# A hybrid block on one core: the x standardisation issued ahead of the magnitudes, and two VectorE side steps issued one head later

## What is computed

```python
def attention_a(x, Wq, Wk, Wv, Wo):          # x: (16, 512, 256), 16 heads of 16
    q, k, v = (split_heads(x @ W.T) for W in (Wq, Wk, Wv))
    scores = einsum('bhqd,bhkd->bhqk', q, k) * 16 ** -0.5
    scores = where(head_mask, scores, finfo.min)   # heads 0-7 strided, heads 8-15 fixed
    out = einsum('bhqk,bhkd->bhqd', softmax(scores), v)
    return out @ Wo.T

def ffn(x, w_gate, w_up, w_down):            # 256 -> 704 -> 256
    h = silu(fp4(x) @ fp4(w_gate).T) * (fp4(x) @ fp4(w_up).T)
    return fp4(h) @ fp4(w_down).T

def fp4(x):       # blocks of 16 along the last dimension
    scale = max(max(abs(block)) / 6, 1e-12)
    return nearest_of_grid(abs(block) / scale) * sign(block) * scale
    # grid: 0, 0.5, 1, 1.5, 2, 3, 4, 6

x = x + attention_a(layernorm(x)); x = x + ffn(layernorm(x))
x = x + attention_b(layernorm(x)); x = x + ffn(layernorm(x))
```

## Time and profile before

| | |
|---|---|
| runs of the kernel before | 3655.23, 3663.86, 3664.30 us (median 3663.86) |
| the profiled execution: its own time, its span | 3658.47 us, 3656.7 us |
| busy in the span: PE, DVE, ACT, POOL | 86%, 76%, 60%, 31% |
| attention A | about 45 to 1120 us |
| first feed-forward | about 1200 to 1770 us |
| attention B | about 1770 to 3065 us |
| second feed-forward | about 3150 to 3656 us |

### The profile page before, as it was taken

How to read it: one execution, slowest core, us unless ns; L and a number is a source line. 1 busy time by engine, 2 the same in 40 slices (tenths; PEclk the granted TensorE clock), 3 DMA queues, 4 the chain that set the end, 5 groups by cost and what they waited for, 6 DMA issues and landing times. The chain is left out here.

```text
span 3656.7 us, 70567 instructions
## 1 busy us (share of the span) xinstructions
PE 3141.8 (86%) x24024; PEld 2441.3 (67%) x24024; DVE 2772.7 (76%) x7209; ACT 2187.4 (60%) x5360; POOL 1121.8 (31%) x664
## 2 busy tenths in 40 slices
PE   6899899899895899997588888888888886699998
PEld 4666666666664788887356565566665654688888
DVE  4676676676666788886488888888878887688887
ACT  4666667676672344433477777877777775344343
POOL 1000000000003455554233333444333333455554
PEclk9999999999996999999699999999999897899999
DMA  5344244244332100000334344443443443110000
GB/s 89 43 68 61 43 68 61 44 68 61 51 49 75 47 18 18 18 12 29 52 50 68 59 69 66 68 72 59 64 71 59 69 60 87 41 35 30 29 30 24
DMA packets 134183, 190.46 MB, mean 52 GB/s; under 512 B 15127, under 2 KB 81559, under 8 KB 133143
## 3 DMA queue, kind: packets, MB, share of 16 engines
q1 hardware_dynamic: 133830, 185.95, 29.9%
HBM read 45.65 MB, written 28.84 MB: 20 GB/s over the span
## 5 line engine op out<-in xcount | busy, mean ns | idle before, releaser
L407 ACT ACTIVATE a_probs<-a_probs,a_negmax 128x176 f32<-128x176 f32 (+4 forms) x1024 | 501.7, 490 | 331.6 <-DVE a_negmax L330 331.2
L330 DVE CUSTOM_DVE_ANT_0 a_probs<-a_mask,a_score 128x176 f32<-128x176 f32 (+4 forms) x1024 | 404.0, 400 | 222.4 <-PE a_score L481 90.2
L492 PE MATMUL a_turned<-ident,a_probs 128*128 128x128 f32 (+1 forms) x2176 | 427.7, 289 | 79.3 <-DVE a_pT L339 71.6
L1716 DVE CUSTOM_DVE_ANT_0 b_u<-b_u,b_score 128x512 f32<-128x512 f32 x512 | 340.4, 681 | 137.2 <-PE b_score L1971 134.8
L1841 ACT ACTIVATE b_u<-b_u,b_negmax 128x512 f32<-128x512 f32 x512 | 367.0, 717 | 113.6 <-DVE b_negmax L1716 112.2
L1245 PE MATMUL f_y_bank<-f_wdT,f_hqT 128*128 128x256 f32 x1536 | 374.7, 396 | 60.2 <-ACT f_hqT L1184 60.2
L1708 DVE SCALAR_TENSOR_TENSOR b_u<-b_u,b_score 128x1024 f32<-128x1024 f32 x256 | 310.1, 1215 | 94.2 <-ACT b_u L1834 91.7
L1245 PEld LDWEIGHTS f_y_bank<-f_wdT,f_hqT 128*128 128x128 f32 x1536 | 296.4, 197 | 108.5 <-issue 67.9
L1834 ACT ACTIVATE b_u<-b_score 128x1024 f32<-128x1024 f32 x256 | 262.3, 1025 | 163.3 <-PE b_score L1961 163.0
L1177 ACT ACTIVATE f_h_mag<-f_hu 128x704 f32<-128x704 f32 x128 | 101.4, 792 | 421.2 <-POOL f_hu L1060 421.2
L1980 PE MATMUL b_turned<-ident,b_u 128*128 128x128 f32 x2048 | 322.1, 282 | 24.7 <-DVE b_pT L1722 19.4
(11 more groups left out here) (236 smaller groups left out, 7160.5 us busy)
## 6 DMA issues: line engine op xcount, KB each, us to landing
b_stack<-b_part SPq DMA_DIRECT2D x192, 256.0 KB, 8.4
a_stack_q<-a_part SPq DMA_DIRECT2D x192, 128.0 KB, 4.3
a_stack_k<-a_part SPq DMA_DIRECT2D x192, 128.0 KB, 5.7
xs<-in_x_dram SPq DMA_DIRECT2D x16, 512.0 KB, 8.2
x_before_b<-xs SPq DMA_DIRECT2D x16, 512.0 KB, 2.9
b_xin<-x_before_b SPq DMA_DIRECT2D x16, 512.0 KB, 12.2
b_xres<-x_before_b SPq DMA_DIRECT2D x16, 512.0 KB, 3.8
x_after_b<-b_xres SPq DMA_DIRECT2D x16, 512.0 KB, 5.8
```

Of the source, the lines that this page charges most:

```text
L330: dve.tensor_tensor_reduce(out=probs[:, n % 2, j, 0:keys(n)], in0=mask_of(n), in1=score[j][:, 0:keys(n)], scale=-1.0, scalar=3.0e38, op0=A ...
L407: act.activation(probs[:, n % 2, j, 0:keys(n)], probs[:, n % 2, j, 0:keys(n)], ACT.Exp, bias=negmax[:, n, j:j + 1], scale=-1.0, accum_out= ...
L492: m = nc.tensor.transpose(turned[j % 2][0:rows, u, :], chunk(n, probs[:, n % 2, j, :], u), ident[:])
L1716: dve.tensor_tensor_reduce(out=u[:, n, j, :], in0=u[:, n, j, :], in1=score[:, j, :], scale=-0.05, scalar=3.0e38, op0=ALU.add, op1=ALU.min, ...
```

## The change

Nothing is added or removed. In attention A, VectorE's share of the jobs Q, K and R is issued at head j = 2 instead of j = 1, behind `mask_max` and `move_turned` of that head; its share of V, y and xT1 stays at j = 1, and ScalarE's share of all jobs stays at j = 1. In both feed-forwards, ScalarE issues `magnitude` as the last part of a step, behind `scalar_magnitude` (n = 0) and `scalar_standard` (n = 2).

```diff
--- before.py
+++ after.py
@@ -363,7 +363,9 @@
-                        job = jobs.get(n - 1, "-") if j == 1 else "-"
+                        job = jobs.get(n - 1, "-")
+                        if j != (2 if job[0] in "QKR" else 1):
+                            continue
                         if job[0] == "R":
                             move_out(sequence(s, job), int(job[1]))
                         elif job[0] in "QKVy" or job == "xT1":
@@ -1191,12 +1193,12 @@
                     if behind(3):
                         move_hidden(*behind(3))
-                    if behind(1):
-                        magnitude(*behind(1))
                     if n == 0 and has(s + 1):
                         front.scalar_magnitude(act, s + 1)
                     if n == 2 and has(s + 2):
                         front.scalar_standard(act, s + 2)
+                    if behind(1):
+                        magnitude(*behind(1))
```

## The result

| | before | changed |
|---|---|---|
| median | 3660.21 us (3655.23 to 3664.3, 4 runs) | 3561.33 us (3557.49 to 3562.71, 4 runs) |
| ratio, 95% interval | | 0.9726 (0.9711 to 0.9741) |
| profiled execution | 3658.5 us | 3560.0 us |
| mean granted clock of its span | 0.927 | 0.944 |

Before's median has one more run in it than the table ahead, made beside the changed kernel's. The change saves 99 us (2.7%), where 42 were predicted. 3561 us is outside the predicted range (3575 to 3655), on its fast side. The direction was right and the size was not.

What follows compares the result with a forecast made beforehand. It took VectorE's order to bound attention A, and the round of GpSimd, ScalarE and VectorE per tile the feed-forward. Terms of 31 + 11 = 42 us off 3658.5 us gave 3616 us, range 3575 to 3655.

Steps and rivals of the forecast that it cites:

- attention A, order, per sequence: Attention A: issuing VectorE's low parts and divisions later saves 2.1 us a sequence, 31 us over 15 sequences.
- groups 12 and 14: Attention A, Q1 and K1: head 2's mask step and copy run during ScalarE's high part, saving 2.2 us a sequence.
- the divisions (groups 1 and 9): Attention A, R1 and R0: head 2's steps fill VectorE's wait for `rsb`, 0.4 us gained in R1, 0 in R0.
- the late K0 part (group 8): Attention A: K0's low part falls behind head 2's copy, so R0 starts 0.8 us late; net loss 0.5 us a sequence.
- Q0 (group 7): Attention A: head 2's two steps fit into the gap before ScalarE's late high part; nothing gained or lost on TensorE.
- feed-forward, order, per sequence: Both feed-forwards: moving ScalarE's magnitudes last gains a net 0.4 us a sequence, 11 us over 28.
- the standardisation (step 2): Feed-forward: x standardisation moves into ScalarE's 5.84 us of idling, so VectorE's stretch between roundings shortens by 1.29 us.
- the x magnitudes (step 0): Feed-forward: put ahead of the tile's magnitudes, they wait for GpSimd's `f_xu` and delay VectorE's rounding, losing 0.9 us a sequence.
- half-clock stretches: Short TensorE stretches at the lower clock: number taken as unchanged, range widened by ten, 18 us, on the fast side.
- The larger gain: Rival, both stages: the waits go whole and late hand-overs are hidden, 92 us off, 3567 us; chance 0.17.
- The slower rival: Both stages: late hand-overs decide, and the gaps in groups 12 and 14 become waits for ScalarE; 3696 us, chance 0.10.
- The no-change case: Rival: x standardisation isn't ready to run early, so the time stays within measurement, 3652 to 3675 us; chance 0.13.

## Why the prediction was right in direction and wrong in size

| step of the prediction | predicted | measured | where from |
|---|---|---|---|
| attention A, order, per sequence | 2.1 us | 1.94 us | 65.10 with gaps filled, 63.16 changed |
| of it groups 12 and 14 | 2.2 | 2.39 | 65.10, and 62.71 with Q1 and K1 alone moved |
| of it the divisions (groups 1 and 9) | 0.4 | 0.33 | divisions put back |
| of it the late K0 part (group 8) | -0.5 | -0.57 | K0's part put back |
| of it Q0 (group 7) | 0 | -0.20 | Q0's part put back |
| feed-forward, order, per sequence | 0.4 | 0.44 | 31.56 before, 31.11 changed |
| of it the standardisation (step 2) | 1.3 | 1.36 | 31.56 before, 30.20 alone |
| of it the x magnitudes (step 0) | -0.9 | -0.91 | 30.20 without their move |
| half-clock stretches | unchanged | 53 us gained | gaps filled; sequence times |

**The step that failed is the clock's.** I wrote that both sequences of the earlier trace rows have the same waits, so that rows can't tell when the clock falls, and took the number of stretches as unchanged. In the earlier trace rows the stretches are there; it is the count that I held fixed. The clock makes 15 times 2.32 (4.26 less 1.94), 35 us, in attention A. In the feed-forwards eleven sequences of before are 1.5 to 1.7 us longer than 31.56, 18 us together, and none is after. That is 53 us that the sum had at nothing, and for which the range held 18. TensorE's busy time agrees: 53.5 us less for the same 24,024 instructions in the profile.

The order makes 15 times 1.94, 29 us, in attention A, and 26.5 less 18.3, 8 us, in the feed-forwards: 37 us, where the sum had 42. The terms were right to 0.2 us each. The two gaps brought more than predicted, since TensorE's wait fell by 1.20 us each (1.41 to 0.21) and not by ScalarE's 1.09. But a feed-forward's 0.44 us doesn't come 28 times: the sequence behind the first x rounding is longer than before (32.37 against 31.36 us, and 32.63 against 31.85), and the last one of each is hardly shorter. What is left has no experiment of its own: 3.0 us at the start and the end of attention A, attention B's 3.8 us and 1.3 us at the start of the second feed-forward.

It could have been read before the run. The earlier trace rows compare whole sequences, in which one short stretch is diluted to a clock of 0.95. The rows around the gap have 0.60 right behind it, and 1.00 ahead of it. That a gap is not always followed by a fall made me call the fall unreadable; it is only uneven, and the question was whether falls occur without gaps. In the kernel with the gaps filled they hardly do: two in the 13 sequences of attention A, and none that lengthens a feed-forward sequence. Why the clock falls behind one gap and not behind the next stays open.

The Trainium skill (TensorE: Matmul & The Clock Gate, HAM oscillation) describes this pattern: TensorE idles, falls back to the lower clock, and pays the way up again for every tile. That section's advice on which idle gaps to avoid names only longer ones than this kernel has. This case's trace disagrees with that part: the gaps were 1.41 and 2.03 us, and filling them removed nearly all of the falls.

**Point by point, what was to show it.** VectorE's wait for `a_part` fell to 4.8 us, under the 15 given; the two waits left are at the stage's start and not in groups 7 or 8. The 1.41 us before the transposes are 0.21. R0 is late by what was said: before, it starts 0.11 us behind the end of the transposes just ahead of it (559.69; the earlier trace rows show the head before those), and now

```profile
526.02 0.66 PE L462 MATMUL a_side<-ident,a_rec 128*128 128x128 f32 x4 [0.86 <-DVE a_part L304]
```

it waits 0.86 us for the low part. For the feed-forward the changed kernel's VectorE has, from step 2 to step 0 that follows:

```profile
1410.87 0.89 DVE L1128 SCALAR_TENSOR_TENSOR f_h_mark<-f_h_mag,f_h_mark 128x704 f32<-128x704 f32 x1
...
1413.84 0.84 DVE L1112 TENSOR_SCALAR f_nscale<-f_amax 128x44 f32<-128x44 f32 x1
...
1417.47 0.83 DVE L1125 SCALAR_TENSOR_TENSOR f_h_mark<-f_h_mag,f_hu 128x704 f32<-128x704 f32 x1
...
1425.89 0.89 DVE L1125 SCALAR_TENSOR_TENSOR f_h_mark<-f_h_mag,f_hu 128x704 f32<-128x704 f32 x1 [0.81 <-issue]
```

From the end of rounding tile 1 (1411.76) to rounding tile 2 (1417.47) it takes 5.71 us, where I had worked out 5.77 from 7.06. The next step has the new wait for ScalarE's magnitudes, 0.81 us (0.7 to 0.9 given). The profile names no releaser for it, but these magnitudes run from 1425.03 to 1425.81, and the rounding starts 0.08 us behind them. A sequence without a clock stretch takes the 31.1 us given. The scale operation takes 0.84 us in step 3 where "0.4 or more" stood. That length costs nothing extra: it begins 2.08 us behind the rounding's end and ends 2.92 us behind it, and in the earlier trace rows, at 0.40 us, it begins at 2.52 and also ends at 2.92. In both places its end is about 0.04 us behind that of GpSimd's division (1414.63 here, below), so an earlier VectorE is only held longer.

```profile
1413.25 1.38 POOL L1062 TENSOR_TENSOR f_hu<-f_hid,f_inv 128x704 f32<-128x704 f32 x1
```

The same thing makes the sequences of 32.0 us. In the only one that the changed kernel has (3404.03 to 3436.03, in the second feed-forward) the clock is 1.00 throughout, and the second small scale operation, 0.17 us elsewhere, starts together with GpSimd's x division and ends 0.04 us behind it:

```profile
3404.10:3436.00 31.90, 30.71 (x185) 28.42 (x184) 30.99 (x52) 13.57 (x23) 17.21 (x12) 1.00 0.11 34
...
3424.57 1.98 DVE L1114 TENSOR_SCALAR f_amax<-f_amax 128x44 f32<-128x44 f32 x1
...
3424.57 1.94 POOL L881 TENSOR_TENSOR f_xu<-f_xh,f_x_inv 128x1024 f32<-128x1024 f32 x1
```

One of the signs to look for was wrong. I expected two shorter waits of TensorE for `f_hqT` in place of one. There is one, in step 1:

```profile
1411.61 2.83 PE L1247 MATMUL f_y_bank<-f_wdT,f_hqT 128*128 128x256 f32 x12
...
1427.57 2.83 PE L1247 MATMUL f_y_bank<-f_wdT,f_hqT 128*128 128x256 f32 x12 [1.10 <-ACT f_hqT L1186]
```

At step 3 (1411.61) only 0.13 us of idling is left. The 1.10 us at step 1 is not followed by a fall: the clock is 1.00 from 1161 to 1601, over 14 sequences.

**The rivals.** The larger gain (3567 us) gave nearly the measured time, for another reason: it let the waits go whole, and they did not (0.86 us before R0, 1.10 us at step 1). A number that fits by a wrong mechanism would have been no better prediction. The slower rival needed ScalarE to be late by itself behind the gap; it runs from the high part into the exponential without idling and TensorE waits 0.21 us, so it doesn't come up. The no-change case needed an x standardisation that isn't ready early: in the changed kernel it starts at 1433.99, right behind ScalarE's moves, is over at 1436.05, and ScalarE then idles 4.12 us before the tile's magnitudes.

## What to carry to other kernels

Where an idle gap of TensorE repeats, read the granted clock in windows of a few microseconds right behind it, not the mean of the stage: here the clock behind the gaps was worth 53 us and the order of the work 37. If the clock falls there, fill the gap with matmuls into a bank that is overwritten anyway, as a test of cause first (55 us here), and then look for the order that closes it. And move only the instruction whose lateness opens the gap: of the six low parts and divisions only Q1's and K1's were needed, and the others together cost more than they brought.

## What the runs showed of the hardware

- The granted clock of TensorE fell to 0.53 and 0.60 (means of windows of 3.6 and 3.4 us) behind idle gaps of only 1.41 us (twice within 10 us, groups 12 and 14) and of 2.03 us. One such stretch cost 1.7 us in the feed-forward (33.25 against 31.56 us a sequence; 4.51 against 2.83 us for the same six matmuls, which show as twelve). In attention A one of 3.6 us cost 0.87 us, and one of 6.8 us 2.37.
- Gaps that stayed in the changed kernel were not followed by falls: 0.86 and 1.05 us in attention A (clock 1.00 from 60 to 1030), 1.10 us in the first feed-forward (1.00 from 1161 to 1601).
- Identical gaps in identical sequences were followed by a costly fall in 11 of 28 sequences of before's feed-forwards, for the most part every second time (1421.2: 0.60; 1454.4: 1.00), and every time once the sequence was 34.14 us long.
- VectorE's small scale operation takes 0.19 us by itself and 0.84 us when it starts while GpSimd divides. In the first feed-forward its mean over 64 goes from 496 to 757 ns, and its end stays tied to GpSimd's. The one behind it took 1.98 us instead of 0.17 when it started together with a GpSimd operation of 1.94 us.
